# Merging paths that share x2's segment and the result's segment in a two-layer graph network, with the path plan made at the start of the program

## What is computed

```python
h = relu(layernorm(x));  x = x + L0(h)
h = relu(layernorm(x));  x = x + L1(h)

def L0(h):  # row, col = edges and self loops; norm = rsqrt(deg[row]) * rsqrt(deg[col])
    return relu(segment_sum(norm[:, None] * (h @ W.T + b)[row], col))

def L1(h):  # x1, x2: (edges, 16, 32)
    x1, x2 = h[src].reshape(-1, 16, 32), edge_attr.reshape(-1, 16, 32)
    contrib = path_coeffs[None, :, None] * x1[:, i1, :] * x2[:, i2, :]
    edge_out = zeros.at[:, i3, :].add(contrib)
    return zeros.at[dst].add(edge_out)
```

## Time and profile before

| | us |
|---|---|
| median of 3 runs | 1053.53 (1052.03 to 1053.58) |
| profiled execution, its own time | 1056.4 |
| its span, first to last instruction | 1054.7 |
| VectorE busy | 896.4 (85%) |
| TensorE matmuls busy | 797.4 (76%) |
| GpSimd busy | 503.4 (48%) |
| ScalarE busy | 444.0 (42%) |
| first product of layer 1 starts at | 291.3 |

### The profile page before, as it was taken

One profiled execution on the slowest core, in us unless ns is written; L12 is line 12 of the kernel. 1 busy time (PEld: TensorE's weight loads), 2 busy tenths in 40 slices (PEclk: granted clock), 3 DMA queues, 4 the chain that ended last, 5 costly groups with the idle time before them and its releaser, 6 DMA issues.

```text
span 1054.7 us, 22852 instructions
## 1 busy us (share of the span) xinstructions
PE 797.4 (76%) x5052; PEld 385.5 (37%) x5053; DVE 896.4 (85%) x2196; ACT 444.0 (42%) x1685; POOL 503.4 (48%) x572
## 2 busy tenths in 40 slices
PE   1688887997057787868788786777878687787868
PEld 0334443443023442524344252433425243442517
DVE  4677668844069999999999999999999999999992
ACT  3888887533501532525152242515224251522422
POOL 4222120344643566666454666646466664646500
PEclk7799999999578988888888888888888878888887
DMA  9000000054464667777665677757567775656610
GB/s 168 1 0 0 0 0 1 1 190 146 140 259 151 219 197 272 259 249 262 212 231 182 249 259 258 260 192 247 181 247 259 259 261 203 244 177 243 231 21 11
DMA packets 59518, 183.05 MB, mean 174 GB/s; under 512 B 20116, under 2 KB 20244, under 8 KB 54972
## 3 DMA queue, kind: packets, MB, share of 16 engines
q0 software_dynamic: 27616, 87.97, 26.8%
q1 hardware_dynamic: 22568, 88.88, 22.7%
q10 hardware_dynamic: 9268, 5.55, 1.9%
HBM read 173.71 MB, written 8.66 MB: 173 GB/s over the span
## 4 chain that ended last, share of the span: by engine, by line
PE 25%; DVEq 22%; DVE 21%; issue 18%; ACT 6%; POOL 4%; DMA 2%; ACTq 1%; SPq 1%; POOLq 0%; another core or an unknown queue 0%
DVE q_mem L861 17%; PE psum L1245 14%; DVEq L853 11%; DVEq L856 6%; PE psum L1228 4%; DVEq L861 4%; PE psum L1145 3%; PE psum L1156 2%; ACT S L1075 2%; DVE x_mem L751 2%; ACT hot_mem L1062 1%; DMA x_mem<-in_L_gnn_W 1%; PE psum L1142 1%; POOL x_mem L620 1%; POOL spare L517 1%
## 5 line engine op out<-in xcount | busy, mean ns | idle before, releaser
L861 DVE TENSOR_TENSOR q_mem<-x_mem 128x448 f32 (+2 forms) x1392 | 724.5, 595 | 49.1 <-DMA x_mem<-h_rows,src_now 31.3
L1245 PE MATMUL psum<-q_mem,hot_mem 128*32 128x512 f32 (+1 forms) x2584 | 392.3, 684 | 158.0 <-DVE q_mem L861 118.9
L620 POOL DMA_INDIRECT x_mem<-h_rows,src_now x323 | 395.9, 1226 | 170.9 <-issue 105.1
L1075 ACT ACTIVATE S<-psum,coef 128x32 f32<-128x32 f32 (+1 forms) x800 | 148.1, 335 | 296.4 <-PE psum L1245 231.4
L1245 PEld LDWEIGHTS psum<-q_mem,hot_mem 128*32 128x32 f32 x2584 | 98.1, 128 | 414.9 <-issue 270.0
L1228 PEld LDWEIGHTS psum<-S,place 128*128 128x128 f32 x1600 | 189.0, 196 | 39.2 <-issue 38.9
L1228 PE MATMUL psum<-S,place 128*128 128x32 f32 x1600 | 196.2, 280 | 7.5 <-issue 7.5
L751 DVE TENSOR_SCALAR x_mem<-x_mem,spare 128x320 bf16<-128x320 f16 x323 | 77.4, 296 | 42.1 <-issue 42.1
L1087 ACT ACTIVATE acc<-psum 128x512 f32<-128x512 f32 x12 | 7.2, 597 | 194.8 <-PE psum L1228 194.8
L1156 PE MATMUL psum<-x_mem,hot_mem 128*128 128x320 bf16 x323 | 67.1, 321 | 28.9 <-DVE x_mem L751 18.8
L969 ACT ACTIVATE hot_mem<-x_mem,spare 128x128 bf16<-128x128 f16 x240 | 74.9, 388 | 20.2 <-PE psum L1156 19.7
(11 more groups left out here) (187 smaller groups left out, 454.4 us busy)
## 6 DMA issues: line engine op xcount, KB each, us to landing
x_mem<-in_edge_attr SPq DMA_DIRECT2D x60, 768.0 KB
x_mem<-in_edge_attr SPq DMA_DIRECT2D x35, 1024.0 KB
x_mem<-h_rows,src_now POOLq DMA_INDIRECT x323
out<-acc POOLq DMA_DIRECT2D x12, 256.0 KB, 4.2
x_mem<-in_x SPq DMA_DIRECT2D x1, 2304.0 KB
out<-x_mem ACTq DMA_DIRECT2D x9, 256.0 KB
h_rows<-x_mem ACTq DMA_DIRECT2D x9, 256.0 KB, 2.0
x_mem<-in_L_gnn_W SPq DMA_DIRECT2D x1, 1024.0 KB, 13.6
```

Of the source, the lines that this page charges most:

```text
L620: pool.indirect_dma_start(x1[:, j * TB + t, :], None, h2_dram[:, :], bass.IndirectOffsetOnAxis(ap=now, axis=0)).then_inc(landed, 16)
L861: return nc.vector.tensor_tensor(q[s % 2][:, 0:tiles, p % PG:p % PG + 1, :], x1_segs[:, first:first + tiles, ds(a, 1), :], x2_segs[:, firs ...
L1075: last = nc.scalar.activation(S[:, p * U:(p + 1) * U], sums, ACT.Copy, scale=coef[:, p:p + 1])
L1245: last = nc.tensor.matmul(ps[s % G][side * M:(side + 1) * M, first * U:end * U], hot[:, j * TB + k, :], q[s % 2][:, k, first:end, :].rearr ...
```

## The change

Besides the repeated pairs, up to EXTRA = 4 paths are merged with an earlier path of the same i2 and i3: their coefficients times their x1 segments are added up once per node, as one of four extra segments of the h2 row, and one product with x2's segment does for both. Rows of h2 in DRAM and of x1 in SBUF grow from 512 to 640 elements. `kept_n` becomes 64 - 6 - 4 = 54.

The plan is no longer made by GpSimd but by VectorE (`merge_paths`, in front of its work on the edge indices), with TensorE summing over the paths in six round trips; the three path DMAs are issued first. VectorE packs it later (`pack_paths`, between the feature parts and `place_items`). In the second layer norm `combine_segments(c - 1)` stands between the variance and the reciprocal of block c, and the h2 rows of block c - 1 are stored from ScalarE's queue one block later. The selection of paths, the packing and the two helper functions are in the diff; the removed code of GpSimd (some 95 lines) and the memory layout are cut.

```diff
...
+    EXTRA = 4
+    WIDE = D + EXTRA * U
...
-    h2_dram = nc.dram_tensor("h2_rows", (N, D), fp32).ap()
+    h2_dram = nc.dram_tensor("h2_rows", (N, WIDE), fp32).ap()
...
-            sp.wait_ge(pads_set, 5)
+            sp.dma_start(path_cols_i, paths).then_inc(paths_in, 16)
+            sp.dma_start(path_vals[:, 3:4], coeffs.rearrange("(n a) -> n a", a=1)).then_inc(paths_in, 16)
+            sp.dma_start(path_rows_i, paths.rearrange("(a n) c -> a (n c)", a=1).broadcast_to([NP, NP * 3])).then_inc(paths_in, 16)
+            sp.wait_ge(pads_set, 3)
...
-            sp.dma_start(path_vals[0:NP, 4:5], coeffs.rearrange("(n a) -> n a", a=1)).then_inc(paths_in, 16)
-            sp.dma_start(path_cols_i[0:NP, :], paths).then_inc(paths_in, 16)
-            sp.dma_start(path_rows_i, paths.rearrange("(a n) c -> a (n c)", a=1).broadcast_to([P, NP * 3])).then_inc(paths_in, 16)
...
-            pool.wait_ge(g_ready, 1)
-            pool.wait_ge(paths_in, 48)
-            steps = [0]
-
...
-                pool.wait_ge(xs_stored, 16 * C)
...
+                        pool.wait_ge(xs_stored, 16 * C)
...
+            def merge_paths():
...
+                def ask(ins):
+                    asked[0] += 1
+                    ins.then_inc(paths_asked, 1)
+                    dve.wait_ge(paths_summed, asked[0])
+                    dve.sem_inc(vector_steps, 1)
...
+                nc.vector.scalar_tensor_tensor(pair_col, i1, float(SEGS), i2, ALU.mult, ALU.add)
+                link(nc.vector.scalar_tensor_tensor(goal_col, i3, float(SEGS), i2, ALU.mult, ALU.add))
+                nc.vector.tensor_scalar(same_pair, pair_row, pair_col, None, ALU.is_equal)
+                link(nc.vector.tensor_scalar(same_goal, goal_row, goal_col, None, ALU.is_equal))
+                nc.vector.tensor_tensor(earlier_goal, same_goal, later, ALU.mult)
+                ask(nc.vector.tensor_tensor(earlier_pair, same_pair, later, ALU.mult))
+
+                nc.vector.tensor_scalar(dropped[:, 0:1], sums[:, 0:1], 1.0, None, ALU.min)
+                ask(nc.vector.tensor_scalar(alone, sums[:, 1:2], 1.0, None, ALU.is_equal))
+
+                nc.vector.tensor_scalar(head, sums[:, 2:3], 0.0, alone, ALU.is_equal, ALU.mult)
+                ask(nc.vector.tensor_scalar(dropped[:, 1:2], sums[:, 2:3], 1.0, alone, ALU.is_equal, ALU.mult))
...
+                link(nc.vector.tensor_scalar(limit, sums[:, 6:7], -1.0, float(LATE), ALU.mult, ALU.add))
+                link(nc.vector.tensor_scalar(limit, limit, 0.0, float(EXTRA), ALU.max, ALU.min))
+                nc.vector.tensor_scalar(dropped[:, 0:1], sums[:, 4:5], float(LATE), dropped[:, 0:1], ALU.is_lt, ALU.mult)
+                link(nc.vector.tensor_scalar(merged[:, 0:1], sums[:, 5:6], limit, dropped[:, 1:2], ALU.is_lt, ALU.mult))
...
+                link(nc.vector.tensor_tensor(place_at, number, sums[:, 12:13], ALU.subtract))
+                link(nc.vector.scalar_tensor_tensor(back, sums[:, 12:13], kept, place_at, ALU.add, ALU.subtract))
+                link(nc.vector.scalar_tensor_tensor(spread, back, gone, place_at, ALU.mult, ALU.add))
+                link(nc.vector.tensor_scalar(shown, gone, -1.0, 1.0, ALU.mult, ALU.add))
+                ask(nc.vector.tensor_tensor(shown, shown, spread, ALU.mult))
...
+                link(nc.vector.tensor_tensor(new_coef, merged[:, 0:1], taken[:, 0:1], ALU.add))
+                link(nc.vector.tensor_scalar(new_coef, new_coef, -1.0, 1.0, ALU.mult, ALU.add))
+                link(nc.vector.scalar_tensor_tensor(new_coef, new_coef, c, taken[:, 0:1], ALU.mult, ALU.add))
+                first_seg = back
+                link(nc.vector.tensor_scalar(first_seg, i1, -1.0, float(SEGS), ALU.mult, ALU.add))
+                link(nc.vector.scalar_tensor_tensor(first_seg, first_seg, taken[:, 0:1], i1, ALU.mult, ALU.add))
+                link(nc.vector.tensor_tensor(first_seg, first_seg, taken[:, 1:2], ALU.add))
+                for k, val in enumerate((first_seg, i2, i3, path_vals[:, 4:5], new_coef)):
+                    nc.vector.tensor_scalar(by_place[:, k * NP:(k + 1) * NP], across, spread, val, ALU.is_equal, ALU.mult)
+                nc.vector.tensor_copy(n_kept, kept[0:1, :])
...
+                ask(last)
+                nc.vector.tensor_copy(laid, ps[3][:, 0:5 * NP + 4 * EXTRA])
...
+                    pack_paths()
                     place_items()
...
+            def combine_segments(c):
+
+                s = c % 2
+                dve.wait_ge(h2_ready, c + 1)
+                for n in range(EXTRA):
+                    last = nc.vector.tensor_scalar(scaled_segs[:, n:n + 1, :], h2_segs[:, s, ds(extra_segs[0][n], 1), :],
+                                                   extra_coefs[0][:, n:n + 1], None, ALU.mult)
+                link(last)
+                for n in range(EXTRA):
+                    last = nc.vector.scalar_tensor_tensor(h2_segs[:, s, SEGS + n:SEGS + n + 1, :], h2_segs[:, s, ds(extra_segs[1][n], 1), :],
+                                                          extra_coefs[1][:, n:n + 1], scaled_segs[:, n:n + 1, :], ALU.mult, ALU.add)
+                last.then_inc(extra_ready, 1)
+
...
                 nc.vector.tensor_scalar(rs2[:, c % 2, 0:1], mv2[:, 1:2], EPS, None, ALU.add).then_inc(var_ready, 1)
+                if c >= 1:
+                    combine_segments(c - 1)
                 dve.wait_ge(root_ready, c + 3)
                 nc.vector.reciprocal(rs2[:, c % 2, 0:1], rs2[:, c % 2, 0:1]).then_inc(xs_ready, 1)
...
+            combine_segments(C - 1)
...
+            def store_rows(c):
+                rows = P if c < C - 1 else LAST
+                act.wait_ge(extra_ready, c + 1)
+                act.dma_start(h2_dram[c * P:c * P + rows, :], h2[0:rows, c % 2, :]).then_inc(h2_stored[c % 2], 16)
...
                 act.dma_start(out[c * P:c * P + rows, :], xs[0:rows, c, :]).then_inc(xs_stored, 16)
-                act.wait_ge(h2_ready, c + 1)
-                act.dma_start(h2_dram[c * P:c * P + rows, :], h2[0:rows, c % 2, :]).then_inc(h2_stored[c % 2], 16)
+                if c >= 1:
+                    store_rows(c - 1)
+            store_rows(C - 1)
...
+            pe.wait_ge(paths_asked, 1)
+            nc.tensor.matmul(sums[:, 0:1], earlier_pair, ones_col, start=True, stop=True)
+            nc.tensor.matmul(sums[:, 1:2], same_pair, ones_col, start=True, stop=True).then_inc(paths_summed, 1)
+            pe.wait_ge(paths_asked, 2)
+            nc.tensor.matmul(sums[:, 2:3], earlier_goal, alone, start=True, stop=True).then_inc(paths_summed, 1)
...
+            pe.wait_ge(paths_asked, 6)
+            nc.tensor.matmul(ps[3][:, 0:5 * NP + 4 * EXTRA], ones, by_place, start=True, stop=True).then_inc(paths_summed, 1)
```

277 lines of the change are left out of this document (128 added, 149 removed).

## The result

The changed kernel takes 1078.0 us (median of 4 runs, 1075.2 to 1078.6) against 1053.55 before: ratio 1.0227, 95% interval 1.0204 to 1.0251. The forecast was 1056.3 with a range to 1068. It is slower by 24.5 us, nine times the forecast difference. The profiled execution took 1078.6, its span is 1076.9, 22.2 more than before.

What follows compares the result with a forecast made beforehand. Two nearly equally long loops bound it, VectorE's own and one over TensorE and ScalarE; only the first shortens. Steady -4.2 plus start 7.0 gave +2.8: 1056.4 to 1059.2, less 2.9 for the median, 1056.3 us; range 1043 to 1068.

Steps and rivals of the forecast that it cites:

- Two loops of nearly equal length: In the items: VectorE's own work and a loop over TensorE and ScalarE; the change shortens the first only.
- the steady part: Items: 50 us of products removed, almost all turning into VectorE waiting for TensorE; -4.2 us, bounds 0 and -8.8.
- the start with what follows it: Before the first gather: plan +8.2, packing +.5, norm +4.3; +6.7 reach that gather, +7.0 with wider rows.
- The turned-round form of rival B: Items: TensorE's slot 2 runs at 1.2 GHz in most items, +1.7 x 11, 1075 us; chance .05.
- rival B: Items: slot 6 leaves TensorE's low-clock stretch, an item gets 1.6 us shorter, 1039 to 1047; chance .20.
- The path plan: Program start: the plan on VectorE ends at 22.0, so line 702 comes at 29.8; +8.2 us, bounds +3.5 and +12.
- The counting of edges: Behind the plan, before layer 1: starts later by the plan's +8.2 us, with no further cost.
- Packing and the layer norm: Before the first gather: packing +.5 us (0 to 3.1) and second norm +4.3 (0 to 9).
- The first gather: GpSimd's first gather moves from 270.25 to 276.9: of 13.0 us added before it, 6.7 arrive.
- rival D: Start: linked instructions on fresh code take .45 and questions 2 us, +10, all on the path, 1066 us; chance .10.
- Wider rows cost nothing: Gathers moving 25% more bytes: room hides the landing, issue stays 1.51 us; only the first gather pays, .3.
- F: Items: issuing a gather of wide rows takes 2.1 us, adding 2.1 an item, 1079 us; chance .04.

Runs made afterwards that it cites:

- the cleanest pair: The kernel before with ScalarE's step moved (1069.5 us, ratio 1.0008), and the same with 4 products fewer in each half (1097.3 us, ratio 1.0285).
- group 3: The changed kernel itself, run on another chip beside variants with ScalarE's step moved: ratio 1.0651 to the kernel before.
- group 4: The changed kernel with half 1's edge loads held back and ScalarE's step, GpSimd's memset and the combining moved: ratio 1.0295 to the kernel before.

## Why the prediction was wrong

**What bounds the kernel.** Two loops of nearly equal length, VectorE's and that over TensorE and ScalarE, was right as far as it went: VectorE's saved time shows as waits of 2.3 and 2.9 (about 2 and 3 were forecast), and 48 us less of VectorE give nothing (run with fewer products). The time forecast from it, 2.8 us more, failed at two terms: the steady part, and the start with what follows it. By the Trainium skill ("Perfetto Trace Analysis", Identifying the Most-Contended Engine) VectorE, the engine of highest occupancy, would be the one to optimize first; the measurements decide against that rule here. Moving ScalarE's step showed that its part is on that loop.

**"Steady part: -4.2"** was +12.4, the other way. The step that failed is the loop over TensorE taken as a fixed length, in which only the margin of VectorE's slot 3 counts and every item gains .35. On the first chip three of eleven items had slot 5 at 1.2 GHz where that loop ended last, 3.2 us each or 9.5 in all; and the other eight gained nothing (61.5 against 61.25). In these TensorE's slot 0, after longer waits than before, takes 5.9 to 6.3 where it took 5.4 to 6.0. The turned-round form of rival B had the right kind of event, but priced it at slot 2 and at a chance of .05; it was slot 5, at 3.2 an item instead of 1.7, since the mixing behind it slows too. The trace of the kernel before had such a slot 5 (409.58), in an item where it cost nothing, and the prediction passed over it. The bounds of the steady part (-8.8 to 0) had no value above zero, though rival B's row of the clock gave no reason to leave one out. On the other chips late signals of slot 7 were added to this, of which the prediction had nothing.

**"The path plan": +8.2** was +17.1. What failed is that the plan was priced as if nothing stood in front of or beside it. Its first answer came at 20.92 and not at 10.1, 10.8 later: 7.7 of that is the late iota, which no row of before could show, and 3.1 the stop beside the memset, which takes 5.5 to 6 on the spot. From there to the plan's end it took 11.5 where 11.9 was reckoned, so the 38 instructions and the questions were priced well; no row of before has the copy of 336 elements at the .5 that this sum gives it, and it took .51 (line 654). The work behind the plan took 6.3 and not 7.84, since GpSimd's wait of 1.47 was gone. Together these make the 8.9.

**The counting of edges** was taken to start later and no more. It also took 3.6 longer for the same matmuls, at a clock of .86 instead of .95, a term that the sum put at nothing. The run of the changed kernel with its path DMAs later takes 143.4 us at .96 there, on another chip, so this isn't bound to the change.

**"Packing and the layer norm": +4.8** was 7.3. The packing cost nothing: the first y starts 36.32 after the reduction in both kernels. The norm was +7.3 and not +4.3: a block grew from 4.53 to 5.14, .6 against the .38 reckoned, mostly since the combining takes 1.36 and not 1.05. That it covers the wait for the root was right.

**"The first gather": of 13.0 added, 6.7 arrive**: the slack of 6.3 was right, 28.5 less 22.2. Every further us counted, as rival D said; D's 1066 was the nearest of the rivals in kind, from other causes.

**"Wider rows cost nothing"**: no issue grew to 1.9 (1.20 + .30, some 1.30 + .30), so F didn't come. Whether more bytes make the stops at the turn longer is open.

**The first item** wasn't in the sum at all. The stops of its first products were in the trace of before, 10 us that belong to no edit; that they were gone in the profiled run was luck. Had the changed kernel kept them there, its span would have been some 32 us longer than before (22.2 and 10.2).

**What stays open.** How transfers make the signal of slot 7 late on the other chips, why the changed kernel has none of this on the first at the same DMA share, and why the kernels with less work for VectorE are hit harder. The same kernel shows the same items on two chips (67.6, 66.3, 67.4, 67.6 and 66.4 in both, to .1), so it is a repeated pattern and no chance. A guess is that VectorE's last product releases the edge loads 2 us earlier against the turn of the other engines; the holds of loads and gathers point there, but they were not tried on the changed kernel as it stands, nor on the kernel before without ScalarE's step. Open too are the cause of the late iota, what lowers the clock in the counting and before slot 5, and why the chips differ.

## What to carry to other kernels

Work taken from the busiest engine turns into its waits when another loop is as long, and such waits are not neutral: they move transfers and other engines' idle time, and here slower matmuls came with them (+3 us an item, three times); in the cleanest pair 48 us less for VectorE came with 28 us more in all. Where two loops are within 1 us of each other, price a moved wait in both directions, from the rows of the same work at either clock. Where a wait in the code looks met for long, look at when its signal was recorded and not only at when the instruction ended. And price work that is moved to another place beside what runs there: a 5.5 us memset of GpSimd made five small VectorE instructions stand still until it ended.

## What the runs showed of the hardware

- VectorE's 64x64 comparisons and 64x1 sums took 5.4 to 6.0 us beside GpSimd's memset of 128x6560, and .14 to .47 without it.
- A slot of 26 matmuls takes 3.63 us at 2.4 GHz and 5.33 at 1.2 GHz, and 32 small mixing matmuls 3.76 and up to 4.83. The slow slots came after waits of 2 to 8 us, but fast ones stand after waits of 3.2 as well.
- The signal of slot 7's last matmul was recorded up to 10.5 us after the end of that matmul in the profile (changed kernel, group 3: 453.82 and 463.41), with a DMA share of .95 to 1.04 around it, and by a median of 6.0 with the loads alone held back (group 4); ScalarE, waiting for it, went on .02 later. With all transfers at that place held back it was recorded within .04, and so it was on the first chip at a DMA share of 1.0.
- The same kernel took 1078 us on one chip and 1137 on two others; the kernel before 1053 on the first and 1062 to 1071 on the others.
